# The causal mask of diagonal score tiles: from a TensorE matmul per tile to a second seed row made by GpSimd

## The reference

```python
xn = layernorm(x)                                        # (2048, 256)
k, q, v = (einsum('ihd,bpd->biph', W, xn) for W in (W_K, W_Q, W_V))      # 16 heads of 128
scores = einsum('biph,biqh->biqp', k, q)
masked = scores * mask - 1e10 * (1 - mask)               # mask = tril(ones): key p <= query q
attn = softmax(masked / sqrt(128), axis=-1)
s = einsum('df,bqf->bqd', W_O, z_flat)                   # z = attn @ v, all heads side by side
g = silu(xn @ W_base.T + b_base + 2 * routed_low_rank(xn))   # the best of 8 experts, rank 16
out = x + s * g
```

## Time and profile before

| | |
|---|---|
| median of 3 runs | 1423.0 us (1422.2 to 1423.47) |
| the profiled execution, its own time | 1423.18 us |
| its span, first to last instruction | 1421.4 us |
| busy share of the span: PE, PEld, DVE, ACT, POOL | 98%, 82%, 85%, 77%, 60% |
| mean granted clock of TensorE | 0.99 |
| mask matmuls (L761) | 256 |

### The profile page before, as it was taken

How to read it: one execution, slowest core, us unless ns; L and a number is a source line. 1 busy time by engine, 2 the same in 40 slices (tenths; PEclk the granted TensorE clock), 3 DMA queues, 4 the chain that set the end, 5 groups by cost and what they waited for, 6 DMA issues and landing times.

```text
span 1421.4 us, 22882 instructions
## 1 busy us (share of the span) xinstructions
PE 1386.3 (98%) x7532; PEld 1169.3 (82%) x7532; DVE 1208.4 (85%) x2605; ACT 1089.7 (77%) x2260; POOL 850.2 (60%) x688
## 2 busy tenths in 40 slices
PE   5899999999999999999999999999999999999996
PEld 4688888888888888888888888888888888888775
DVE  6688998889898988889988898989888899888964
ACT  2578886888778787788868887787877888688851
POOL 3265675557666575666755576665756667555850
PEclk9799999999999999999999999999999999999998
DMA  2110001000100000100010001001011000100002
GB/s 81 31 31 16 14 10 46 8 16 16 31 23 9 23 16 23 30 16 12 13 45 9 16 16 31 24 8 23 14 25 31 16 10 14 36 15 16 16 31 89
DMA packets 30070, 33.73 MB, mean 24 GB/s; under 512 B 11008, under 2 KB 17664, under 8 KB 29952
## 3 DMA queue, kind: packets, MB, share of 16 engines
q1 hardware_dynamic: 29952, 32.26, 9.1%
HBM read 30.02 MB, written 2.23 MB: 23 GB/s over the span
## 4 chain that ended last, share of the span: by engine, by line
PE 94%; DVE 3%; DMA 1%; ACT 1%; issue 1%; SPq 0%; DVEq 0%; ACTq 0%
PE ps L295 27%; PE ps L297 26%; PE ps L296 26%; PE ps L749 9%; PE ps L784 2%; PE ps L761 1%; DVE p_lo L579 1%; PE ps L812 1%; DVE partmax L593 1%; PE ps L702 0%; DMA acc<-x_dram 0%; DVE acc L571 0%; PE ps L718 0%; DVE stats L549 0%; DMA spread<-max_dram 0%
## 5 line engine op out<-in xcount | busy, mean ns | idle before, releaser
L448 POOL TENSOR_TENSOR colsum<-colsum,probs 128x512 f32<-128x512 f32 (+3 forms) x512 | 661.8, 1293 | 207.4 <-ACT probs L526 167.9
L579 DVE TENSOR_TENSOR p_lo<-probs,p_hi 128x512 fp32r<-128x512 f32 (+3 forms) x640 | 537.5, 848 | 13.7 <-ACT p_hi L527 13.6
L526 ACT ACTIVATE probs<-ps 128x512 f32<-128x512 f32 (+3 forms) x640 | 346.1, 541 | 145.1 <-PE ps L297 83.8
L503 ACT ACTIVATE ps<-maxrow 128x512 f32<-128x512 f32 (+3 forms) x640 | 356.2, 557 | 0.0
L527 ACT ACTIVATE p_hi<-ps 128x512 fp32r<-128x512 f32 (+3 forms) x640 | 345.7, 540 | 0.0
L593 DVE TENSOR_REDUCE partmax<-ps 128x1 f32<-128x512 f32 x384 | 256.5, 681 | 3.0 <-PE ps L749 0.3
L295 PE MATMUL ps<-p_hi,v_hi 128*128 128x512 f32 (+3 forms) x640 | 239.4, 374 | 1.4 <-DVE p_lo L579 0.9
L295 PE MATMUL ps<-qT_hi,kT_hi 128*128 128x512 f32 (+3 forms) x640 | 236.3, 369 | 3.6 <-ACT ps L503 3.6
L749 PE MATMUL ps<-kT_hi,qT_hi 128*128 128x512 f32 (+3 forms) x640 | 233.9, 388 | 1.7 <-DVE qT_lo L587 1.0
L297 PE MATMUL ps<-p_hi,v_lo 128*128 128x512 f32 (+3 forms) x640 | 233.2, 364 | 0.0
L296 PE MATMUL ps<-qT_lo,kT_hi 128*128 128x512 f32 (+3 forms) x640 | 233.0, 364 | 0.0
(11 more groups left out here) (108 smaller groups left out, 2232.7 us busy)
## 6 DMA issues: line engine op xcount, KB each, us to landing
spread<-max_dram SPq DMA_DIRECT2D x64, 256.0 KB, 3.8
wraw<-wqk_dram SPq DMA_DIRECT2D x16, 256.0 KB, 4.2
acc<-x_dram SPq DMA_DIRECT2D x4, 512.0 KB, 6.8
wraw<-wv_dram SPq DMA_DIRECT2D x8, 256.0 KB, 4.8
wraw<-wo_dram SPq DMA_DIRECT2D x8, 256.0 KB, 3.3
probs<-x_dram SPq DMA_DIRECT2D x4, 512.0 KB, 4.5
out_dram<-acc SPq DMA_DIRECT2D x4, 512.0 KB, 2.9
max_dram<-rowmax SPq DMA_DIRECT2D x64, 2.0 KB, 1.4
```

The lines of the kernel that those rows point to most:

```text
L448: nc.gpsimd.tensor_tensor(total[:, c0:], total[:, c0:], tile[:, c0:], ALU.add)\
L503: nc.scalar.activation(st[job.n % SCORE_BANKS][:, c0:], maxrow[:, job.g, c0:], ACT.Copy)\
L526: nc.scalar.activation(probs[:, k, c0:], src, ACT.Exp, scale=SCALE).then_inc(probs_ready, 1)
L579: nc.vector.tensor_tensor(p_lo[:, k, c0:], probs[:, k, c0:], f32(p_hi[:, k, c0:]), ALU.subtract)\
```

## The change

- TensorE no longer adds the mask. The bf16 identity and mask, and GpSimd's instructions that made them, are gone.
- A second row of seeds, `masked`, takes its place. For each block (head and group) GpSimd takes the ordered row `maxrow` and puts -1e10 wherever the query is in front of the key, in all four 128-column parts at once (`mask_maxima`, one affine select of 128x512). Two such rows alternate. It waits for the ordering of the block, and for the seeds of the block two before.
- ScalarE seeds a diagonal tile in two instructions: the first 128 columns from `masked`, the rest from `maxrow` as before (a tile of 128 columns has the first only). It waits for the block's masked row.
- `mask_at` puts the select into GpSimd's queue: six tiles ahead of the block's first diagonal tile, but not before its ordering, in front of that tile's column sum.
- `masked` lies in the second half of the buffer `gate`. The scratch product of the masked row maximum, which lay in `gate` too, now goes back to the PSUM bank that it comes from.
- `SCHEDULE` is another order of the same jobs.

```diff
+MASK_AHEAD = 6
...
-    "w V10 Pk02 V00 w M0202 Pk03 V01 w z7 | s7 | Pq03 | o70 M0222 v | v o71 M0311 | v M0212 S0 | M0232 v M0313 "
-    "M0321 | v V11 M0333 V21 v Z0 | M0320 v M0332 | M0330 M0301 | O00 v v M0302 M0303 | v O01 M0322 | v M0300 | "
...
+    "w V00 Pk02 V10 w M0202 Pk03 M0212 w z7 V01 s7 | Pq03 | o70 o71 | v M0222 | M0311 v | v M0232 | S0 v M0313 "
+    "V31 M0320 | Z0 V11 V21 v M0302 | M0321 M0303 v | v M0332 M0301 | O00 v | v v O01 M0322 | v | M0330 M0331 v "
+    "M0300 v M0310 | M0323 Z1 | V20 | M0333 v | Pk11 M0312 v v | Pq10 | Pq11 v S1 | Pk10 v v | M1120 M1110 v "
+    "M1131 | | O10 v M1000 O11 | v | S2 v M1130 | v | v v M1121 | v M1111 M1020 Z2 V30 | Pq12 | v M1010 v M1100 | "
...
-        ident_bf = sb("ident_bf", [P, P], BF16)
-        mask_bf = sb("mask_bf", [P, P], BF16)
...
-        masked_row = gate[:, :, :, :].rearrange("p a t d -> p (a t d)")[:, 0:AUX_BANKS * BW]\
-            .rearrange("p (k n) -> p k n", k=AUX_BANKS)
+        masked = gate[:, 1].rearrange("p t d -> p (t d)").rearrange("p (k n) -> p k n", k=2)
...
+        mask_at = []
+        for block, gi in enumerate(max_blocks):
+            head, g = divmod(gi, NB)
+            diagonal = first_tile[gi] + TB * g
+            mask_at.append(max(order_at[block], diagonal - MASK_AHEAD))
...
-            nc.gpsimd.memset(ident_bf[:, :], 0.0).then_inc(made, 1)
-            nc.gpsimd.memset(mask_bf[:, :], 0.0).then_inc(made, 1)
...
-            nc.gpsimd.affine_select(out=ident_bf[:, :], in_=ident_bf[:, :], fill=1.0, **diagonal)
-            nc.gpsimd.affine_select(out=mask_bf[:, :], in_=mask_bf[:, :], compare_op=ALU.is_ge, fill=MASKED,
-                                    base=0, pattern=[[1, P]], channel_multiplier=-1)
...
-            his = 2
+            def mask_maxima(block):
+
+                pool.wait_ge(max_ordered, block + 1)
+                if block >= 2:
+                    pool.wait_ge(seeded, tiles_until(max_blocks[block - 2]))
+                nc.gpsimd.affine_select(out=masked[:, block % 2, :].rearrange("p (t n) -> p t n", t=TB),
+                                        in_=maxrow[:, max_blocks[block] % NB, :].rearrange("p (t n) -> p t n", t=TB),
+                                        compare_op=ALU.is_ge, fill=MASKED, base=0, pattern=[[0, TB], [1, P]],
+                                        channel_multiplier=-1).then_inc(max_masked, 1)
+
+            his, masks = 2, 0
             for job in plan:
                 if not isinstance(job, Score):
                     continue
                 n, c0 = job.n, columns(job)
                 gi = job.head * NB + job.g
+                while masks < len(max_blocks) and mask_at[masks] <= n:
+                    mask_maxima(masks)
+                    masks += 1
...
-                c0 = columns(job)
-                nc.scalar.activation(st[job.n % SCORE_BANKS][:, c0:], maxrow[:, job.g, c0:], ACT.Copy)\
-                  .then_inc(seeded, 1)
+                dst, c0, plain = st[job.n % SCORE_BANKS], columns(job), columns(job)
+                if job.kt // TB == job.g:
+                    block = max_blocks.index(job.head * NB + job.g)
+                    plain = c0 + P
+                    act.wait_ge(max_masked, block + 1)
+                    op = nc.scalar.activation(dst[:, c0:plain], masked[:, block % 2, c0:plain], ACT.Copy)
+                if plain < BW:
+                    op = nc.scalar.activation(dst[:, plain:], maxrow[:, job.g, plain:], ACT.Copy)
+                op.then_inc(seeded, 1)
...
-                            out=masked_row[:, k, 0:w], in0=src[:, 0:w], in1=mask_rows[:, BW - w:], scale=1.0,
+                            out=src[:, 0:w], in0=src[:, 0:w], in1=mask_rows[:, BW - w:], scale=1.0,
...
-                    if job.kt // TB == job.g:
-                        op = nc.tensor.matmul(dst[:, 0:P], ident_bf[:, :], mask_bf[:, :], start=False, stop=True,
-                                              skip_group_check=True)
```

More of the change, by code:

```diff
@@ L26 @@
 F32R = mybir.dt.float32r
-BF16 = mybir.dt.bfloat16
 P = 128
@@ L246, in attention_layer @@
         max_ordered = sem("max_ordered")
+        max_masked = sem("max_masked")
         bits_set = sem("bits_set")
@@ L283, in attention_layer @@
                 order_at.append(tile and min(tile - 1 + ORDER_LAG, first_tile[job.head * NB + job.g] - SEED_AHEAD))
+        mask_at = []
[3 more added lines that the diff above has]
+            mask_at.append(max(order_at[block], diagonal - MASK_AHEAD))
+        assert mask_at == sorted(mask_at) and max_blocks == sorted(max_blocks)
         def columns(t):
@@ L413, in _ @@
                 nc.gpsimd.memset(rank[:, :, e:e + 1], float(E - e))
-            pool.wait_ge(made, 5)
+            pool.wait_ge(made, 3)
             diagonal = dict(compare_op=ALU.not_equal, base=0, pattern=[[-1, P]], channel_multiplier=1)
             nc.gpsimd.affine_select(out=ident[:, :], in_=ident[:, :], fill=1.0, **diagonal)
-            nc.gpsimd.affine_select(out=ident_bf[:, :], in_=ident_bf[:, :], fill=1.0, **diagonal)
-            nc.gpsimd.affine_select(out=mask_bf[:, :], in_=mask_bf[:, :], compare_op=ALU.is_ge, fill=MASKED,
-                                    base=0, pattern=[[1, P]], channel_multiplier=-1)
             nc.gpsimd.affine_select(out=mask_rows[:, BW - P:], in_=mask_rows[:, BW - P:], compare_op=ALU.is_ge,
```

## The result

The changed kernel takes 1414.4 us (median of 4, 1413.6 to 1414.76) against 1422.96 (median of 4 beside it): a ratio of 0.994, 95% interval 0.9922 to 0.9957. It is faster by 8.6 us, which is small but clear of the noise; 1393.0 was forecast, and 1414.4 lies above the range.

What follows compares the result with a forecast made beforehand. TensorE was taken as the only bound from 100 to 1322 us. 1423.2 - 31.5 (mask matmuls) + 1 (last pair) + 0.3 (start) = 1393.0 us, range 1387 to 1400, chance 0.75.

Steps and rivals of the forecast that it cites:

- What bounds the kernel now.: From 100 to 1322 us TensorE alone bounds; VectorE, ScalarE and GpSimd have 20.6, 31.6 and 61.4 us slack a pair.
- up to 5 us of waits at TensorE: Allowance in the forecast's range for TensorE waiting as VectorE rises from 88% to 90% of the pair.
- The price of the mask matmul.: On TensorE, removing 256 mask matmuls at 0.123 us each saves 31.5 us, 3.9 per pair.
- the waiting seed: Rival, chance 0.05: at group 0 of each head the select comes behind another colsum pass; 26 us return, 1419.
- half the price: Rival, chance 0.09: 0.08 us stays with the matmul behind each mask matmul, so only 14 us go: 1409.
- Split seeds.: ScalarE's 192 extra seed instructions on diagonal tiles add 2.2 us a pair, 18 us in all, beside TensorE.
- Masked row.: GpSimd's 64 affine selects take 0.75 us each, 6 us a pair, covered by idle time; no cost from new waits.
- Product in PSUM.: VectorE's masked maxima take 0.01 us more each, 2.5 us in all, hidden in VectorE's 20.6 us of slack.
- The other order.: Same jobs in another schedule: TensorE's sum unchanged, -3 to +4 us at its edges, taken as nothing.
- Nothing shrinks: Rival, chance 0.05: VectorE's 20.6 us of waits in a pair remain, so the period stays 166 us: 1423.
- VectorE through PSUM: Rival, chance 0.06: 256 masked maxima slowed by PSUM writes, 10.7 us a pair; with rigid waits 86 us more, 1509.
- Last pair.: With GpSimd loaded by feed-forward weights, a 0.75 us mask select comes in a stretch without gaps: about 1 us late, once.

Runs made afterwards that it cites:

- short sums: Changed kernel with GpSimd's column-sum passes cut to the first 128 columns, sums of the other columns left out: 1389.8 us, 161.9 us a pair.
- half passes: Changed kernel with each of GpSimd's column-sum passes cut in two at column 256, same sums: 1416.5 us, ratio 0.9916.
- product in SBUF: Changed kernel with the product of the masked row maximum going to SBUF scratch rows again: 1414.7 us, ratio 0.995.
- four maxima to tile 0: Changed kernel with four row maxima moved from tiles 72 and 73 of a pair to tile 0 of the next: 1425.6 us.
- three maxima earlier: Changed kernel with three row maxima moved from tiles 75 and 77 of a pair to tiles 64, 65 and 67: 1413.7 us.
- old order with half passes: Changed kernel with the schedule of the kernel before and each GpSimd column-sum pass cut in two: 1414.9 us, ratio 0.994.

## Why the prediction was wrong, step by step

- *What bounds the kernel now.* "TensorE is the only bound from 100 to 1322 us" was the failing step, with the sentence behind it, that the span shortens until one of the slacks in a pair is used up. A slack counts where the wait is. VectorE was full in the last 16 us of each pair before, which one query by stretches would have shown; I took the mean of the pair. From this followed the too small term "up to 5 us of waits at TensorE": a pair came out 2.7 us longer than forecast, 19 us in seven pairs, and the run with short sums puts 2.6 us a pair at the very tiles where TensorE waits for VectorE. Of VectorE's rise, the 6.5 us a pair of p_lo's hold-up was in no term of the sum.
- *The price of the mask matmul.* A little high: 0.11 us a tile in the median where VectorE is out of the way, against 0.123, and 2.9 us a pair of the 3.9 when it alone is taken out. The 161.9 us a pair with short sums, against 162.0, is a match of the whole in which the order, the seeds and the selects have their part too. Two rivals came nearest to the time, the waiting seed (1419) and half the price (1409), and both are wrong in their mechanism: no wait for the masked row is listed, and the runs in which only the mask matmuls differ show 17 to 22 us for all of them. The rule weighed beside it, in the Trainium skill's "VectorE: DVE Perf Modes", section on the TRN2 errata, makes 56 ns each and 14 us in all (an estimate), and all three pairs of runs show more than that.
- *Split seeds.* Right: 0.301 us each, no effect.
- *Masked row.* Duration right (0.798 for 0.75), its place right (no wait of ScalarE for it in the lists), "covered by idle time" wrong in the old order: GpSimd's time is not only its own, it shifts the passes against p_lo and holds p_lo itself. 1.4 us a pair there; in the new order the kernel without the selects is slower.
- *Product in PSUM.* 0.007 us more a maximum (0.01 forecast); the longer accumulator read behind it, 0.136 for 0.081 us, was not foreseen, but the next instruction starts as early as before (0.61 us). No effect on the time.
- *The other order.* Taken as nothing, bounded by -3 to +4 us. By itself it costs 17, with 7.7 us a pair more of hold-up. The bounds looked at which jobs TensorE does, not at whether VectorE's p_lo starts before or behind a pass.
- *Nothing shrinks*, the rival with VectorE's waits rigid, had the right engine; of its 20.6 us 12.9 are left (164.7 - 151.8). *The seed waits for GpSimd* did not happen. *VectorE through PSUM* did not happen.
- *Last pair.* +1 us was forecast on top of -3.9; it took 0.6 less than before in all.

Open: why the new order is better with the selects than without them, and better in the changed kernel than with the mask merely left out; what the 0.6 us a pair are that the old order loses when the shared path is free; and what makes the clock fall in the last pair.

## What to carry to other kernels

Before counting an engine's slack as cover, read its busy time in stretches of a tenth of the repeating unit: a queue that is full at one place gives nothing from elsewhere. Where a VectorE instruction has two SBUF inputs and GpSimd reads SBUF beside it, count the hold-up as part of the instruction's price; here cutting GpSimd's passes in two helped more than moving VectorE's work. Price an instruction by what starts behind it: the length of the accumulator read says nothing. An order fitted by hand is fitted to durations; after a change of one engine's time it is to be measured alone as well.

## What the runs showed of the hardware

- p_lo behind a running GpSimd pass ends 0.55 us after the pass, whatever was left of it; ahead of the pass it takes 0.68 us, and the pass ends 1.15 us after it, 1.56 us long in the median (1.66 in the row shown) instead of 1.29.
- A GpSimd select of 512 columns, with one SBUF input, holds p_lo the same way: 31 cases, 0.54 us from its end to p_lo's.
- A wait of TensorE for p_lo costs 0.11 us more than its length, at the following matmul (0.34 us from start to start in place of 0.23).
- The accumulator read behind a VectorE maximum takes 0.136 us when the product goes to PSUM, 0.079 to 0.081 when it goes to SBUF; the next instruction starts 0.61 us after a maximum of 512 columns in either case.
- The granted clock fell to half for 31 us of the last pair in the profiled execution of the half passes; it and the five like it took 14 us longer than the other four. It fell for 10 us in the last pair in the profiled executions of four other runs (product in SBUF, four maxima to tile 0, three maxima earlier, old order with half passes).
